# ScalarE instead of SP issues the transfers of the rows of maxima in a cross-attention and expert-FFN kernel

## The chip, the cores and the metric

The kernel runs on one core of one Trainium2 chip. The metric is the device time of one execution in microseconds; less is better. A comparison of two kernels takes the median of several executions of each on the same chip.

## What is computed

The reference handles 8 batches of 512 positions with 256 features. Each batch goes through two stages, each added to its input:

- **An mLSTM cross-attention** with 4 heads of 64: gates from products with the inputs, a cumulated log forget gate, a running maximum, and a decayed product of queries, keys and values.
- **A feed-forward block.** Its first half is a mixture of two multi-head attentions (M = 2, H = 16 heads of KD = 16 each, so 32 heads). For each head it computes

```
scores = q k^T / sqrt(16)        # 512 x 512
attn   = softmax(scores, axis=-1)
ctx    = attn v
```

Its second half picks two of eight experts for the batch and applies them (`gelu(n2 w1) w2`).

The change is about the softmax of the 32 heads. The softmax needs, for each query position, the maximum of its 512 scores. The kernel computes all scores twice: first with queries on the partitions, to take maxima along the free axis, and then with keys on the partitions, where the maximum of a query has to be subtracted in each column.

## The kernel before, in words

**Heads, quads, slots.** Heads are handled four at a time: a quad. A batch has `NQ` = 8 quads. For every quad, TensorE makes 16 tiles of scores with queries on the partitions (`maximum`, line 851), and VectorE reduces each to a column of maxima (line 1378). Then TensorE transposes the 16 columns to 16 rows (`max_rows`, line 859, shown as line 452 of the helper), and VectorE writes them negated, as a high and a low bf16 part, to `mrow` (lines 1386 and 1388). Two DMAs of 4 KB per quad copy these rows from 16 partitions of `mrow` into two rows of the operand `qst` (`send_rows`, line 2009). With these two rows, the second product (`score`, line 866: 98 contraction rows, the last two against ones) comes out of TensorE with the maximum already subtracted, and ScalarE only has to exponentiate it (`exponent`, line 1677) into `prob`. TensorE multiplies `prob` with the values (line 881).

One batch is a **period** of 128 **slots**; a slot is one score tile and one exponential. The scores of quad `qq` use slots 16·`qq` to 16·`qq`+15. A period takes about 167 us here (period 5 runs from 901.6 to 1068.9 us).

**Written-out order.** Each engine has its own program, written out by hand slot by slot. In each period four things run beside the slots: the maxima of the quads to come (the string `AHEAD` says how many tiles per slot), the first stage of the next batch (`stage_a`), the second half of the projections of this batch (`second_half`), and the end of the previous batch with its experts (`stage_c`). Tables such as `ACT_A` and `SP_C` give the slot of each piece on each engine. There are three plans: `FIRST` for period 0, `MIDDLE` for periods 1 to 6, `LAST` for period 7.

**When rows are made and sent.** `rows_at(plan, later)` finds the slot in which the sixteenth maximum of a quad is made and adds `later`. TensorE and VectorE do `max_rows` at `LATER` = 1 slot behind it, and the send stands at `LATER + SENT` = 2 slots behind it. In `MIDDLE` the sends stand at slots 14, 24, 44, 62, 76, 89, 102 (for quads 1 to 7) and 123 (for quad 0 of the next batch). In `FIRST`: 10, 23, 33, 45, 71, 88, 103, 123. In `LAST`: 13, 20, 38, 60, 72, 85, 105.

**SP's queue.** SP issues every DMA of the kernel, 613 in all, strictly in program order, each behind its semaphore waits: the inputs (line 1941), the three parts of the projections into their stacked places in `kst` and `qst` (`stack`, line 1954, twelve DMAs of 128 KB for a pair of pieces), the gates' rows, the expert weights (lines 2025, 2032), the results, and the maxima rows. The first score of a quad waits for the rows:

```
if g == 0 and j == 0:
    e.wait_ge(rows_in[q_ % 2], 32 * (q_ // 2 + 1))
```

**PSUM banks.** Seven banks (`RB`) are taken in turn by everything TensorE makes, in TensorE's program order (`take`). A tile can start only when the engine that reads the tile seven takes earlier in the same bank has let it go (`u.free`). So a reader that is late on one tile stops TensorE seven tiles later, whatever that tile is for.

**ScalarE's program** around a slot is, in this order: the exponential of the slot, then pieces of `second_half`, `stage_c` and `stage_a` that stand at the slot, then (once per quad) the copy of the quad's context (line 1685). Pieces that matter here: `grow0` of `stage_a` (line 1498, reads the tile of the gates, made at line 502), the copies of values (line 1587), and in the last period `copy_columns` (line 1635).

Of the kernel before, what the change touches and what calls it, by code (L numbers as in the profile page):

```python
# [90 lines left out]
def build(nc, d, out):  # L91

    B, S, E = d["x"].shape
# [11 lines left out]
    QUAD = 4  # L105
    NQ = M * H // QUAD
# [3 lines left out]
    KROWS = len(TERMS_K) * KD  # L110
# [4 lines left out]
    with ctx:  # L115
        def sb(name, shape, dt=F32):
            return ctx.enter_context(nc.sbuf_tensor(name, shape, dt))

        def sem(name):
            return ctx.enter_context(nc.semaphore(name))  # L120
# [43 lines left out]
        rows = mid[0:NH].rearrange("p (r s) -> p r s", r=3)  # L164
# [17 lines left out]
        qst = sb("qst", [P, M * H, S], BF16)  # L182
# [6 lines left out]
        mrow = sb("mrow", [QUAD * NT, 2, 2, P], BF16)  # L189
# [73 lines left out]
        rows_in = [sem("rows_in_0"), sem("rows_in_1")]  # L263
# [24 lines left out]
        uses = ring.uses  # L288
# [6 lines left out]
        LATER, SENT = 1, 1  # L295
# [83 lines left out]
        def periods():  # L379

            for b in range(B):
                plan = FIRST if b == 0 else LAST if b == B - 1 else MIDDLE
                yield b, (b - 1 if b > 0 else None), (b + 1 if b + 1 < B else None), plan
# [10 lines left out]
        def behind_maxima(a, first):  # L394

            a.upto(TILES)
            first.upto(-5)
            a.rest()
            first.upto(-2)
# [10 lines left out]
        def place(plan, slot):  # L410

            return sum(map(int, plan["AHEAD"][:slot]))
# [6 lines left out]
        def rows_at(plan, later):  # L419

            return {next(s for s in range(SLOTS) if place(plan, s + 1) >= TILES * q) + later: (q // NQ, q % NQ)
                    for q in range(1, NQ + 1)}
# [1050 lines left out]

        @block.scalar
        def scalar_program(e):
            def stage_a(b):
                for c in range(KC):
                    yield f"kT{c}"
                    u = uses["kT", b, c]
                    e.wait_ge(u.full, u.n)  # L1480
                    e.activation(kT[:, c, :], psum[:, u.bank, :], ACT.Copy).then_inc(u.free, 1)
                for c in range(KC):
                    yield f"qT{c}"
                    u = uses["qT", b, c]
# [3 lines left out]
                if b > 0:  # L1488
                    yield "gpart"
                    u = uses["gparts", b]  # L1490
# [3 lines left out]
                u = uses["gates", b]  # L1494
# [12 lines left out]
                for h in range(NH):  # L1507
                    for c in range(NT):
                        yield f"mask{h}{c}"
                        if h == 0 and c == 0:  # L1510
# [3 lines left out]
                            u = uses["cols", b]  # L1514
# [23 lines left out]
                for c in range(KC):  # L1538
                    yield f"n1T{c}"
                    u = uses["n1T", b, c]  # L1540
# [61 lines left out]
            def second_half(b):  # L1602
                if b == 0:
                    yield "p3"
                    high(b, 3)
                for pt in range(NT // 2 if b == 0 else 0):
                    yield f"pv{pt}"
                    copy_v(b, 0, pt)
                for n in range(len(PIECES) // M, len(PIECES)):
                    yield f"p{n}"  # L1610
                    high(b, n)
                for pt in range(NT // 2):
                    yield f"v{pt}"
                    copy_v(b, 1, pt)

            def stage_c(b):
                for m in range(M):
                    for c in range(KC):
                        yield f"cxT{m}{c}"
                        u = uses["cxT", b, m, c]  # L1620
                        e.wait_ge(u.full, u.n)
                        e.activation(cxT[:, m, c, :], psum[:, u.bank, :], ACT.Copy).then_inc(u.free, 1)
                yield from experts(b)
# [48 lines left out]
            def exponent(b, qq, g, j):  # L1672
                n, u = (b * NQ + qq) * NT + g, uses["score", b, qq, g, j]
                e.wait_ge(u.full, u.n)
                if j == 0 and n > 1:
                    e.wait_ge(valued, n - 1)
                e.activation(prob[:, g % 2, j, :], psum[:, u.bank, :], ACT.Exp).then_inc(u.free, 1)  # L1677
# [12 lines left out]
            until_maxima(a, first)  # L1690
            behind_maxima(a, first)
            for b, behind, ahead, plan in periods():
                a = first if b == 0 else Side(stage_a(ahead) if ahead is not None else iter(()), plan["ACT_A"])
                c = Side(stage_c(behind) if behind is not None else iter(()), plan["ACT_C"])
                v = Side(second_half(b), plan["ACT_S"])
                w = Side(early(b) if ahead is None else iter(()), EARLY_ACT)
                a.upto(-1)
                c.upto(-1)
                for qq in range(NQ):
                    for g in range(NT):  # L1700
                        for j in range(QUAD):
                            slot = (qq * NT + g) * QUAD + j
                            exponent(b, qq, g, j)
                            v.upto(slot)
                            c.upto(slot)
                            a.upto(slot)
                            w.upto(slot)
                            if g == COPY // QUAD and j == COPY % QUAD and b + qq > 0:
                                copy_context(*divmod(b * NQ + qq - 1, NQ))
                if ahead is None:  # L1710
                    copy_context(B - 1, NQ - 1)
                if ahead is not None:
                    c.rest()
                    a.rest()
                else:
                    z = Side(ending(b), ENDING)
                    for slot in range(SLOTS, SLOTS + AFTER):
                        c.upto(slot)
                        z.upto(slot)
# [219 lines left out]
        def sync_program(e):  # L1939
# [65 lines left out]
            def send_rows(b, qq):  # L2005
                u, q_ = uses["rows", b, qq], b * NQ + qq
                e.wait_ge(u.free, u.n)
                for r in range(2):
                    e.dma_start(qst[KROWS + r:KROWS + r + 1, qq * QUAD:(qq + 1) * QUAD, :], mrow[:, q_ % 2, r, :]
                                ).then_inc(rows_in[q_ % 2], 16)  # L2010
# [79 lines left out]
            until_maxima(a, first)  # L2090
            behind_maxima(a, first)
            for b, behind, ahead, plan in periods():
                sends = rows_at(plan, LATER + SENT)
                a = first if b == 0 else Side(stage_a(ahead) if ahead is not None else iter(()), plan["SP_A"])
                c = Side(stage_c(behind) if behind is not None else iter(()), plan["SP_C"])
                v = Side(second_half(b), plan["SP_S"])
                a.upto(-1)
                for slot in range(SLOTS):
                    if slot in sends and b + sends[slot][0] < B:
                        send_rows(b + sends[slot][0], sends[slot][1])  # L2100
                    v.upto(slot)
                    c.upto(slot)
                    a.upto(slot)
                if ahead is not None:
                    c.rest()
                    a.rest()
                else:
                    z = Side(ending(b), ENDING)
                    for slot in range(SLOTS, SLOTS + AFTER):
                        c.upto(slot)  # L2110
                        z.upto(slot)
# [30 lines left out]
```

## Time and profile before

| what | value |
|---|---|
| times of three runs | 1421.33, 1423.33, 1429.55 us |
| median | 1423.33 us |
| span of the profiled execution | 1426.9 us |
| TensorE (PE) busy | 1393.6 us, 98% |
| VectorE (DVE) busy | 1092.2 us, 77% |
| ScalarE (ACT) busy | 916.4 us, 64% |
| GpSimd (POOL) busy | 363.6 us, 25% |
| granted TensorE clock, mean | 0.990 |
| row DMAs (line 2009) | 128 of 4 KB, median 2.1 us from issue to landing |

The page gives no time of the profiled execution beside its span. The span, from the first to the last instruction, lies between the lowest and the highest of the three runs and 3.6 us over their median. In the page, a group of instructions has its busy time, the mean of one in ns, then the idle time of its engine just before it and who ended that. A busy TensorE is not TensorE at its peak, since its matmuls overlap and their ends are modelled: the step from one matmul's start to the next tells more. "SPq" is SP's queue of DMA issues.

### The profile page before, as it was taken

Reading aid. Unit: us, or ns where it says so; the run is one execution under the profiler, and the core shown is the slowest. Engines: PE = TensorE matmul, PEld = TensorE weight load, DVE = VectorE, ACT = ScalarE, POOL = GpSimd, SP = SyncE. Lnnn points to the kernel's source line nnn. Section 1 sums busy time; section 2 is a strip of 40 time slices with the busy share of each in tenths; the row PEclk is TensorE's granted clock in tenths of the full one; section 3 lists DMA queues with packets and bytes.
Section 4 is the critical chain, followed back from the end, with each engine's and each line's share of the span. In section 5 each row is a group of like instructions: output and inputs, shape, how many; then the busy total and the mean of one; then the engine's idle time right before and its main releaser. Section 6 shows DMA issues by size and latency. Waiting matters only on the chain.

```text
span 1426.9 us, 22218 instructions
## 1 busy us (share of the span) xinstructions
PE 1393.6 (98%) x7666; PEld 716.9 (50%) x7666; DVE 1092.2 (77%) x2299; ACT 916.4 (64%) x1706; POOL 363.6 (25%) x351
## 2 busy tenths in 40 slices
PE   8999899999999999999999999999999999999999
PEld 5643434455454654555445554455545454454456
DVE  5779977987789877987779877797769986786721
ACT  3266557766677666675677765876666766757752
POOL 6512342203313123132241133130331322330000
PEclk9999999999999999999999999999999999999999
DMA  4056037430854127441464308541084413561002
GB/s 116 17 70 95 2 45 107 71 62 16 104 76 76 45 38 112 75 75 31 51 101 69 64 31 101 79 75 46 24 102 70 78 56 45 73 77 46 17 1 89
DMA packets 92308, 90.15 MB, mean 63 GB/s; under 512 B 16483, under 2 KB 87267, under 8 KB 91295
## 3 DMA queue, kind: packets, MB, share of 16 engines
q1 hardware_dynamic: 92196, 88.73, 38.6%
q8 instruction: 62, 1.02, 0.3%
q14 instruction: 50, 0.40, 0.1%
HBM read 35.05 MB, written 4.25 MB: 28 GB/s over the span
## 4 chain that ended last, share of the span: by engine, by line
PE 69%; issue 8%; DVE 4%; DMA 3%; SPq 2%; POOL 1%; ACT 1%; DVEq 0%; POOLq 0%; ACTq 0%
PE psum L881 12%; PE psum L866 12%; PE psum L851 12%; PE psum L819 7%; PE psum L838 6%; PE psum L701 5%; PE psum L452 5%; PE psum L736 3%; DMA qst<-mrow 3%; PE psum L475 2%; SPq L1954 2%; PE psum L563 2%; DVE mx L1378 1%; PE psum L573 1%; DVE x L1293 1%
## 5 line engine op out<-in xcount | busy, mean ns | idle before, releaser
L1378 DVE TENSOR_REDUCE mx<-psum 128x1 f32<-128x512 f32 x1024 | 645.5, 681 | 134.2 <-PE psum L851 133.5
L1677 ACT ACTIVATE prob<-psum 128x512 f32<-128x512 f32 x1024 | 568.2, 600 | 270.8 <-PE psum L881 159.4
L866 PE MATMUL psum<-qst,kst 98*128 98x512 bf16 x1024 | 355.9, 383 | 10.5 <-DMA qst<-mrow 8.7
L851 PE MATMUL psum<-kst,qst 96*128 96x512 bf16 x1024 | 318.8, 381 | 2.9 <-DVE resid L1252 1.3
L881 PE MATMUL psum<-prob,vst 128*17 128x512 f32 x2048 | 248.1, 601 | 2.7 <-ACT prob L1677 2.3
L866 PEld LDWEIGHTS psum<-qst,kst 98*128 98x128 bf16 x1024 | 96.9, 99 | 220.8 <-issue 126.9
L851 PEld LDWEIGHTS psum<-kst,qst 96*128 96x128 bf16 x1024 | 99.0, 98 | 121.2 <-issue 17.9
L881 PEld LDWEIGHTS psum<-prob,vst 128*17 128x17 f32 x2048 | 46.7, 97 | 136.3 <-issue 106.8
L838 PE MATMUL psum<-w,cxT 128*128 128x256 f32 x448 | 105.4, 381 | 0.0
L819 PE MATMUL psum<-n2T,x 128*128 128x512 f32 x224 | 103.0, 592 | 0.0
L1828 POOL CAST parts<-resid 128x512 bf16<-128x512 f32 x64 | 41.0, 640 | 239.9 <-DVE resid L1252 239.9
L838 PEld LDWEIGHTS psum<-w,cxT 128*128 128x128 f32 x448 | 85.0, 191 | 16.7 <-DVE acc L1372 1.4
L1748 POOL TENSOR_SCALAR_AFFINE_SELECT cmat<-cmat 128x512 f32<-128x512 f32 x32 | 20.3, 637 | 227.1 <-ACT cmat L1521 227.1
L1830 POOL TENSOR_TENSOR parts<-resid,parts 128x512 bf16<-128x512 f32 x64 | 74.4, 1163 | 5.1
L1798 POOL TENSOR_TENSOR kin<-qbuf,onw 128x1024 f32<-128x1024 f32 (+1 forms) x8 | 16.4, 2054 | 218.2 <-DVE qbuf L1089 216.1
L1724 POOL TENSOR_TENSOR rstd_a<-rstd_a,neghalf 128x4 f32<-128x4 f32 x24 | 25.1, 1055 | 179.4 <-DVE rstd_a L963 109.1
L819 PEld LDWEIGHTS psum<-n2T,x 128*128 128x128 f32 x224 | 42.4, 190 | 39.5 <-issue 34.1
L701 PE MATMUL psum<-n1T,wk 128*128 128x512 f32 x128 | 60.6, 595 | 0.0
L475 PE MATMUL psum<-wv,n1T 128*128 128x256 f32 x256 | 60.5, 379 | 0.0
L701 PE MATMUL psum<-n1T,wq 128*128 128x512 f32 x128 | 60.2, 592 | 0.0
L1599 ACT ACTIVATE parts<-psum,bks 128x512 bf16<-128x512 f32 x32 | 22.0, 687 | 58.4 <-PE psum L701 58.4
L475 PEld LDWEIGHTS psum<-wv,n1T 128*128 128x128 f32 x256 | 48.5, 190 | 9.3 <-ACT prob L1677 0.9
(244 smaller groups left out, 1761.5 us busy)
## 6 DMA issues: line engine op xcount, KB each, us to landing
kst<-parts SPq DMA_DIRECT2D x186, 128.0 KB, 4.7
qst<-parts SPq DMA_DIRECT2D x186, 128.0 KB, 5.9
cmat<-G_dram SPq DMA_DIRECT2D x7, 1024.0 KB, 4.6
x<-in_L_ffn_fw SPq DMA_DIRECT2D x14, 512.0 KB, 3.7
w<-in_L_ffn_fw SPq DMA_DIRECT2D x14, 512.0 KB, 4.2
xbuf<-in_x SPq DMA_DIRECT2D x8, 512.0 KB, 5.1
kin<-in_ctx SPq DMA_DIRECT2D x8, 512.0 KB, 4.5
out<-acc SPq DMA_DIRECT2D x7, 512.0 KB, 9.0
```

What stands on the lines that cost most here:

```text
L452: return e.transpose(out_, in_, ident[0:n, 0:n])
L475: ins = e.matmul(psum[:, u.bank, i * H * KD:(i + 1) * H * KD], n1T[:, kc, t * P:(t + 1) * P], wv[:, kc, m, :], start=kc == 0, stop=kc == K ...
L701: ins = e.matmul(psum[:, u.bank, :], w_[:, kc, m, c * P:(c + 1) * P], n1T[:, kc, :], start=kc == 0, stop=kc == KC - 1)
L736: ins = e.matmul(psum[:, u.bank, 0:E], cxT[:, m, c, t * P:(t + 1) * P], wo[:, m, c, :], start=k == 0, stop=k == M * KC - 1)
L819: ins = e.matmul(psum[:, u.bank, :], w1_of(b, k)[:, kc, f * P:(f + 1) * P], n2T_of(b)[:, kc, :], start=kc == 0, stop=kc == KC - 1)
L838: ins = e.matmul(psum[:, u.bank, 0:E], hidden_of(b, k)[:, f, t * P:(t + 1) * P], w2_of(b, k)[:, f, :], start=f == 0, stop=f == FC - 1)
L851: e.matmul(psum[:, u.bank, :], qst[0:KROWS, h, t * P:(t + 1) * P], kst[0:KROWS, h, :], start=True, stop=True).then_inc(u.full, 1)
L866: e.matmul(psum[:, u.bank, :], kst[0:KROWS + 2, h, g * P:(g + 1) * P], qst[0:KROWS + 2, h, :], start=True, stop=True).then_inc(u.full, 1)
L881: ins = e.matmul(psum[32 * j:32 * j + VW, VB, :], vst[:, g, h, :], prob[:, g % 2, j, :], start=g == 0, stop=g == NT - 1, tile_position=(0, ...
L1378: e.tensor_reduce(mx[:, qq * QUAD + j, t:t + 1], psum[:, u.bank, :], AX, ALU.max).then_inc(u.free, 1)
L1677: e.activation(prob[:, g % 2, j, :], psum[:, u.bank, :], ACT.Exp).then_inc(u.free, 1)
L1830: e.tensor_tensor(parts[:, n % 2, 2, :], resid[:, n % 2, :], parts[:, n % 2, 1, :], ALU.subtract).then_inc(split_lo, 1)
```

## The change

`send_rows` is added to ScalarE's program, with the same wait and the same two DMAs, and stands directly behind the exponential of the slot in which SP had it. SP's loop over slots no longer sends rows. SP keeps the rows of the very first quad, ahead of period 0. Nothing else changes: the number of DMAs, the buffers, the semaphores and all tables of slots are the same.

```
         @block.scalar
         def scalar_program(e):
+            def send_rows(b, qq):
+                u, q_ = uses["rows", b, qq], b * NQ + qq
+                e.wait_ge(u.free, u.n)
+                for r in range(2):
+                    e.dma_start(qst[KROWS + r:KROWS + r + 1, qq * QUAD:(qq + 1) * QUAD, :], mrow[:, q_ % 2, r, :]
+                                ).then_inc(rows_in[q_ % 2], 16)
...
             for b, behind, ahead, plan in periods():
+                sends = rows_at(plan, LATER + SENT)
...
                             exponent(b, qq, g, j)
+                            if slot in sends and b + sends[slot][0] < B:
+                                send_rows(b + sends[slot][0], sends[slot][1])
                             v.upto(slot)
...
         def sync_program(e):
...
-                sends = rows_at(plan, LATER + SENT)
...
                 for slot in range(SLOTS):
-                    if slot in sends and b + sends[slot][0] < B:
-                        send_rows(b + sends[slot][0], sends[slot][1])
                     v.upto(slot)
```

## Rows read from the trace of the kernel before

**Rows 1.** Page, part 1: busy us (share of the span) xinstructions

```profile
PE 1393.6 (98%) x7666; PEld 716.9 (50%) x7666; DVE 1092.2 (77%) x2299; ACT 916.4 (64%) x1706; POOL 363.6 (25%) x351
```

**Rows 2.** Page, part 5: busy us, mean ns | idle before, releaser

```profile
L1677 ACT ACTIVATE prob<-psum 128x512 f32<-128x512 f32 x1024 | 568.2, 600 | 270.8 <-PE psum L881 159.4
L866 PE MATMUL psum<-qst,kst 98*128 98x512 bf16 x1024 | 355.9, 383 | 10.5 <-DMA qst<-mrow 8.7
```

**Rows 3.** TensorE's waits, whole span: us in total, times, longest us

```profile
PE psum L866 <- DMA qst<-mrow: 8.7, 9, 2.9
```

**Rows 4.** The same view from 235 to 1070 us, periods 1 to 5

```profile
PE psum L866 <- DMA qst<-mrow: 4.3, 6, 0.9
```

**Rows 5.** Waits of SP's queue, whole span, same columns

```profile
SPq L2009 <- DVE mrow L1388: 346.1, 51, 28.1
```

**Rows 6.** Line L2009, min/median/max: issue (ns), issue to landing (us)

```profile
L2009 SPq DMA_DIRECT2D qst<-mrow x128: 502/584/1826, 81.0 to 1353.7; - x128
...
DMA to landing us min/median/max: 1.6/2.1/5.8
```

**Rows 7.** Timeline, period 5, slot 89: start us, us, instruction, [idle before]

```profile
1031.46 0.28 DVE L1388 SCALAR_TENSOR_TENSOR mrow<-psum,mrow 16x128 bf16<-16x128 f32 x1
1031.79 3.83 SPq L1954 DMA_DIRECT2D kst<-parts  x6
...
1032.43 2.83 ACT L1677 ACTIVATE prob<-psum 128x512 f32<-128x512 f32 x5 [0.71 <-PE psum L881]
...
1035.67 1.23 SPq L2009 DMA_DIRECT2D qst<-mrow  x2
...
1042.14 0.39 PE L866 MATMUL psum<-qst,kst 98*128 98x512 bf16 x1 [0.88 <-DMA qst<-mrow]
```

**Rows 8.** Timeline of period 5 around slot 14

```profile
921.37 1.05 PE L502 MATMUL psum<-cmat,wsum 128*36 128x512 f32 x2
...
922.35 0.28 PE L452 MATMUL psum<-ident,mx 128*16 128x128 f32 x1
...
922.46 0.38 PE L866 MATMUL psum<-qst,kst 98*128 98x512 bf16 x1
...
922.68 0.81 PE L851 MATMUL psum<-kst,qst 96*128 96x512 bf16 x3
923.04 0.57 ACT L1677 ACTIVATE prob<-psum 128x512 f32<-128x512 f32 x1
...
923.33 3.62 PE L736 MATMUL psum<-wo,cxT 128*128 128x256 f32 x16
923.63 0.68 ACT L1498 ACTIVATE cmat<-psum,gbias 4x512 f32<-4x512 f32 x1
...
924.08 0.28 DVE L1388 SCALAR_TENSOR_TENSOR mrow<-psum,mrow 16x128 bf16<-16x128 f32 x1
```

**Rows 9.** Timeline of period 5 around slot 123

```profile
1064.71 3.16 ACT L1677 ACTIVATE prob<-psum 128x512 f32<-128x512 f32 x6 [0.94 <-PE psum L881]
...
1066.23 0.28 DVE L1388 SCALAR_TENSOR_TENSOR mrow<-psum,mrow 16x128 bf16<-16x128 f32 x1
...
1067.76 0.58 SPq L1941 DMA_DIRECT2D kin<-in_ctx  x1
...
1068.29 0.60 ACT L1587 ACTIVATE vst<-psum 128x512 f32<-128x512 f32 x1 [0.42 <-PE psum L475]
...
1069.31 1.06 ACT L1677 ACTIVATE prob<-psum 128x512 f32<-128x512 f32 x2
...
1069.94 0.09 PEld L866 LDWEIGHTS psum<-qst,kst 98*128 98x128 bf16 x1 [0.29 <-ACT prob L1677]
```

**Rows 10.** Timeline of the last period around slot 85

```profile
1340.10 0.59 ACT L1635 ACTIVATE kin<-psum 128x512 f32<-128x512 f32 x1
...
1340.47 0.28 DVE L1388 SCALAR_TENSOR_TENSOR mrow<-psum,mrow 16x128 bf16<-16x128 f32 x1
...
1340.97 0.60 PE L866 MATMUL psum<-qst,kst 98*128 98x512 bf16 x2
```

More of the change, by code:

```diff
@@ L1475, in scalar_program, with send_rows @@
         def scalar_program(e):
+            def send_rows(b, qq):
+                u, q_ = uses["rows", b, qq], b * NQ + qq
+                e.wait_ge(u.free, u.n)
+                for r in range(2):
+                    e.dma_start(qst[KROWS + r:KROWS + r + 1, qq * QUAD:(qq + 1) * QUAD, :], mrow[:, q_ % 2, r, :]
+                                ).then_inc(rows_in[q_ % 2], 16)
             def stage_a(b):
@@ L1692, in scalar_program @@
             for b, behind, ahead, plan in periods():
+                sends = rows_at(plan, LATER + SENT)
                 a = first if b == 0 else Side(stage_a(ahead) if ahead is not None else iter(()), plan["ACT_A"])
@@ L1703, in scalar_program @@
                             exponent(b, qq, g, j)
+                            if slot in sends and b + sends[slot][0] < B:
+                                send_rows(b + sends[slot][0], sends[slot][1])
                             v.upto(slot)
@@ L2092, in sync_program @@
             for b, behind, ahead, plan in periods():
-                sends = rows_at(plan, LATER + SENT)
                 a = first if b == 0 else Side(stage_a(ahead) if ahead is not None else iter(()), plan["SP_A"])
@@ L2098, in sync_program @@
                 for slot in range(SLOTS):
-                    if slot in sends and b + sends[slot][0] < B:
-                        send_rows(b + sends[slot][0], sends[slot][1])
                     v.upto(slot)
```

## The prediction

> **What bounds the kernel now.** I read the page first. TensorE is busy 98% of the span, VectorE 77%, ScalarE 64% [rows 1]. So a time can only be gained where TensorE stands still, and it is lost wherever ScalarE or a transfer makes it stand still once more. The costliest groups show where ScalarE has room: before its 1024 exponentials it is idle 270.8 us, mostly because TensorE is not ready [rows 2]. The same part shows what the rows of maxima cost today: 8.7 us of TensorE's idle time before `score` ends with their transfer. The view of TensorE's waits says how these lie: nine waits, the longest 2.9 us [rows 3]; six of them with 4.3 us together fall between 235 and 1070 us [rows 4]. This is the largest entry that TensorE has. It is also all that earlier rows can give back.
>
> Why are they late? SP stands in `send_rows` for 346.1 us in all, waiting for VectorE [rows 5], and that is harmless. The timeline around slot 89 shows the harmful case [rows 7]. VectorE ends `mrow` at 1031.74. SP has just begun a stack of six DMAs and reaches the rows at 1035.67, 3.9 us late. They then land behind 128 KB transfers, and the first score of the quad starts at 1042.14, after 0.88 us of idling. The shape is the same in each middle period.
>
> **What the change takes away.** 126 issues leave SP. At slot 89 ScalarE can issue by 1033, since the five exponentials that begin at 1032.43 include that of slot 89 as the second [rows 7]. That is 2.7 us earlier. Even if the rows then still took the 6.4 us from issue to use that they take now (1035.67 to 1042.1), they would be there at 1039.4, before the 1041.2 at which TensorE asks. With the median landing of 2.1 us [rows 6] they are there by 1036. I take all nine waits as gone: **-8.7 us**. The least is 5, if the long one of period 0 (2.9 us) stays in part.
>
> SP runs ahead where it stood in `send_rows`. At slot 123 the loads of the next batch go out at 1067.76, behind the rows [rows 9]; they will go out up to ten microseconds earlier. TensorE does not wait for them now, so nothing is gained: 0. What could be lost is that they share the DMA engines with the rows of slot 123, whose quad starts as they land; 0 to 0.5 us in seven periods. I take 0, because the loads start long enough before the rows to be nearly done.
>
> **What it adds.** A pair of issues occupied SP for 1.18 us (median 584 ns for one [rows 6]; 1.23 in [rows 7]). No row shows ScalarE issuing a DMA. The bounds are 0, if its work in progress covers the issue, and 1.83 us per issue, the longest of SP's. I take SP's 1.18 us a pair, the nearest row, during which nothing behind the pair can begin. 63 pairs make 74 us; as ScalarE waits 270.8 us for TensorE, most of it is hidden by those waits. Without that cover each pair costs its 1.2 us. What counts is where TensorE follows closely on ScalarE. The program order gives these places, and the timeline their slack:
>
> **Slot 14, six middle periods.** Behind the exponential of slot 14 stands the read of the gates' tile, line 1498. It began at 923.63 and ended at 924.31 [rows 8]. The send now stands between them and waits for `mrow`, which ends at 924.36: the change adds a wait here too. Then come 1.18 us, so line 1498 begins at 925.6 and ends at 926.3, 2.0 us late. Who needs it? The gates' bank comes round again seven takes after line 502: the transposed maxima, one score, three maxima, the first product tile of line 736, the second. Sixteen matmul records lie at 0.216 us ((3.62 - 0.38) / 15), eight a tile, so the second tile began at 923.33 + 8 x 0.216 = 925.06. It will begin 0.15 us after 926.3, at 926.45. Loss: 1.4 us, six times: **+8.4 us**. This is the one price that the table of slots hands to the change.
>
> **Slot 123, seven periods.** `mrow` ends at 1066.51, the pair holds ScalarE until 1067.7, and the exponential behind it, which began at 1066.77, begins 1.0 us later. ScalarE's 0.42 us of idling before line 1587 absorbs part, so the exponentials at 1069.31 are 0.5 us late [rows 9]. The next weight load follows straight upon ScalarE (0.29 us of idling ended by it): 0.4 us, seven times: **+2.8 us**.
>
> **Slot 24, six periods.** Here a run of eight exponentials without a gap follows, and 0.75 us of delay (1.18 plus the restart, less the 0.49 us step of exponentials) is carried through it. TensorE gets about half by its seven banks: 0.4 us, six times: **+2.4 us**. This is an estimate from the run of slot 123, not read from a row; its ends are 0 and 0.75.
>
> **Slots 44, 62, 76, 89, 102.** `mrow` is done before the exponential or just as it begins, and ScalarE is then about to wait for TensorE: 0. If the cover is thin, 0.3 us each, 9 us over six periods; that goes into the upper end.
>
> **First and last period.** At slot 85 of the last one, line 1635 begins at 1340.10 and TensorE's matmul at 1340.97 follows 0.28 us behind its end. `mrow` ends at 1340.75, so line 1635 begins at 1342.0, 1.9 us late: 1.8 us on TensorE [rows 10]. Period 0 has two or three tight places of this kind (ends of `mrow` at or behind the exponential at slots 33 and 45), which I put at 1.0 to 1.5 us each by the two places worked out; with small ones in the last period I take 5.6 us for both periods: **+5.6 us**, between 2 and 9.
>
> **Sum:** 8.4 + 2.8 + 2.4 + 5.6 - 8.7 = +10.5 us against the span of 1426.9. The median of the runs is 3.6 us under the span; I put the same difference on the median: 1423.3 + 10.5 = 1433.8, rounded to **1434 us**.
>
> **Against a rule.** The transfers are not the point here; what the issue costs against its transfer is. The pair costs its issuer 1.18 us while the transfer takes 2.1 us [rows 6], so the cost of issuing is more than half of the transfer. The Trainium skill, "DMA: Bandwidth & Descriptors", section "Issuing engines are not separate DMA queues", says that issuing on several engines saves only the sequencer's time, which is usually small relative to the DMA. For 4 KB the trace does not agree with the second half; taken as it stands, that rule would let the +19.2 us vanish and the gain with it shrink to what SP's lateness caused.
>
> **The rivals.**
> *A. ScalarE is not held up.* Work already handed to it goes on while the DMAs are issued, so only the wait for `mrow` is left. Then the prices fall and the 8.7 us stay as gain, less about 4 us for slots 14 and 85, where the wait alone delays lines 1498 and 1635 by 0.7 us: 1423.3 - 8.7 + 4 = 1418.6, and 1414.6 if that is covered as well. For it: runs of exponentials start every 0.5 us although each lasts 0.6 [rows 2], [rows 9], so something is ahead. Against it: most of ScalarE's time before exponentials is spent waiting, so little is in hand, and it cannot begin what has not been handed over. It decides if the pair holds ScalarE for under 0.6 us. The Trainium skill, "Advanced Engine Details and Errata", section "Engine Queue Depths", gives ScalarE a queue of 8, which would favour this rival; no row shows how full it is.
> *B. The issue is dearer on ScalarE,* because SP issues at the same time. At 0.9 us each a pair costs 0.6 more. All the places above (6 + 7 + 6 + about 5) rise by that 0.6, 14 us, less the two microseconds that still hide: 1423.3 + 10.5 + 12 = 1446. For it: the longest issue of SP took 1826 ns [rows 6].
> *C. It comes out even.* The bank order leaves more slack than I count, and slot 14 alone costs: 8.4 + 1.8 - 8.7, or 1425. For it: ScalarE is idle a fifth of the span before exponentials [rows 2].
> *D. The change does nothing,* the rows go out at the same moments. Slot 89 speaks against it; it would give 1423 and falls to C.
>
> **How the numbers follow.** 0.5% of 1423.3 is 7.1 us, about what a measurement of this kernel can tell from no change; so the bounds are 1416.2 and 1430.4. Forecast (1428 to 1440): 0.58. A: 0.14, a third of it below 1416.2. B: 0.12. C and D: 0.16. Faster: 0.05 of A and a little for the unseen, 0.07. Slower: B 0.12, and 0.52 of the forecast's 0.58, 0.64. Same: the rest, 0.29. The range leaves out the low half of A and the high half of B: 1418 to 1446.
>
> **What would show it.** DMA issues of rows on ScalarE's queue of 0.5 to 0.6 us each; no wait of TensorE for `qst<-mrow` at slot 89; line 1498 beginning 2 us later relative to the exponential of slot 14, and TensorE idle before the second tile of line 736 with ScalarE as the releaser; middle periods longer by about 1.2 us each (2.2 lost, 1.0 won). I am wrong if pairs last under 0.6 us or if ScalarE begins work during them, if line 736 has no gap, or if new waits for the rows appear at slot 123.

## The result, and the profile after

| | before | after |
|---|---|---|
| median, same chip | 1422.36 us | 1512.31 us |
| all runs | 1421.33 to 1429.55 | 1510.2 to 1514.29 |
| span of the profiled execution | 1426.9 us | 1510.5 us |
| mean granted TensorE clock | 0.990 | 0.969 |

The ratio is 1.0624, 95% interval 1.06 to 1.0647: slower by 90 us. The forecast was 1434 us, range 1418 to 1446. The direction was right, and the size was off by a factor of eight.

Of the page of after, these lines of parts 1, 3 and 5 (busy us, count; queue, packets, MB, share; busy us, mean ns | idle before, releaser) answer to [rows 1, 2]. The line numbers have moved with the change: the exponential of line 1677 is line 1684 here, the read of the gates' tile 1505 (was 1498), the stacks 1964 (was 1954), the loads 1951 (was 1941), and the send, which was line 2009, is line 1480.

```profile
PE 1423.1 (94%) x7666; PEld 717.2 (47%) x7666; DVE 1089.0 (72%) x2299; ACT 915.3 (61%) x1706; POOL 363.7 (24%) x351
...
q1 hardware_dynamic: 88164, 88.21, 37.8%
q10 hardware_dynamic: 4032, 0.52, 0.3%
...
L1684 ACT ACTIVATE prob<-psum 128x512 f32<-128x512 f32 x1024 | 569.9, 601 | 344.1 <-PE psum L881 203.7
L866 PE MATMUL psum<-qst,kst 98*128 98x512 bf16 x1024 | 359.9, 388 | 51.3 <-DMA qst<-mrow 48.0
```

Two things stand out. The same 7666 matmuls keep TensorE busy 29.5 us longer (1423.1 against 1393.6), while its busy *share* falls from 98% to 94%: it is both slower at its work and idle more. And the wait which the change was to remove has grown from 8.7 to 48.0 us. `q10` is new: 126 of the 128 row transfers are now on ScalarE's own queue.

The view of TensorE's waits (us in total, times, longest) puts two entries ahead of all others; [rows 3] has the first of them before:

```profile
PE psum L866 <- DMA qst<-mrow: 48.0, 16, 4.9
PE psum L736 <- ACT cmat L1505: 7.8, 6, 2.3
```

The second is the price of slot 14, which was forecast. The first was forecast to go to zero. The issues themselves are as cheap as forecast; line 1480 in the view by line (min/median/max of an issue in ns, then of issue to landing in us), against [rows 6]:

```profile
L1480 ACTq DMA_DIRECT2D qst<-mrow x126: 510/604/1766, 103.4 to 1437.5; - x126
...
DMA to landing us min/median/max: 1.6/2.5/9.9
```

So ScalarE issues the rows on time and quickly, and some of them then take up to 9.9 us instead of 5.8 at most. Which ones follows from TensorE's idle time before the first score of each quad. In the six middle periods, 26.9 of the 48.0 us stand before the quad whose rows go out at slot 102 (3.9 to 4.9 us each time) and 13.0 us before that of slot 24 (1.8 to 2.9 us). Another 3.5 and 1.4 us stand before quad 1 of the first and the last period, and 2.8 us before quad 6 of the first period, where the kernel before had 2.9 us already. At slot 123 there is no wait over 0.15 us.

The timeline of period 5 around slot 102 shows such a case (start us, us, instruction, [idle before <- releaser]):

```profile
1109.84 3.78 SPq L1964 DMA_DIRECT2D qst<-parts  x6
...
1111.63 0.28 DVE L1388 SCALAR_TENSOR_TENSOR mrow<-psum,mrow 16x128 bf16<-16x128 f32 x1
...
1111.94 1.31 ACTq L1480 DMA_DIRECT2D qst<-mrow  x2
...
1113.66 0.59 SPq L1951 DMA_DIRECT2D kin<-in_ctx  x1
...
1122.35 0.61 PE L866 MATMUL psum<-qst,kst 98*128 98x512 bf16 x1 [4.77 <-DMA qst<-mrow]
...
1123.18 0.63 PE L866 MATMUL psum<-qst,kst 98*128 98x512 bf16 x1
```

SP started a stack of six 128 KB transfers at 1109.84, 2.1 us ahead of the rows. In the kernel before it was the other way round, since SP itself had to wait for `mrow` and send the rows first. This is the timeline of before at the same slot of the same period:

```profile
1051.43 0.28 DVE L1388 SCALAR_TENSOR_TENSOR mrow<-psum,mrow 16x128 bf16<-16x128 f32 x1
...
1051.74 1.18 SPq L2009 DMA_DIRECT2D qst<-mrow  x2
...
1053.02 3.81 SPq L1954 DMA_DIRECT2D qst<-parts  x6
```

There the two rows took at most 4.2 us to land. In after they took 9.1 and 9.8 us, as the view of line 1480 in this stretch says:

```profile
DMA to landing us min/median/max: 9.1/9.4/9.8
```

The landings lie in the order of issue across the two queues: the stack's fourth transfer, issued at 1111.72 by SP, landed at 1120.99; ScalarE's first row, issued at 1111.94, at 1120.99 too; the stack's fifth, issued at 1112.37, at 1122.01. From one 128 KB transfer to the next about 1.1 us pass, so each of them that goes out ahead of the rows holds them up by about 1.1 us: for the second row, five of them on top of the 4.2 us of the kernel before make 9.7 us, and it took 9.8. (For the first, four on top of 3.5 us make 7.9, and it took 9.1, so the 1.1 us are an estimate.) The Trainium skill, "DMA: Bandwidth & Descriptors", section "Issuing engines are not separate DMA queues", says that DMAs run on the same 16 engines whoever issues them; the trace agrees. The same page of the Trainium skill, section "Queues, rings and completion order", lets each DMA engine take turns between queues, packet by packet. One would expect from it that 4 KB need not wait for a backlog of the other queue; the 9.8 us do not show that. The profile's view of the DMA queues from 1111.9 to 1117.9 us has no packet of `q10` at all, so the rows stood for 6 us before any of their packets moved. Where in the path from the issue to the packets they stood, no run here tells.

Why was TensorE slower at its work as well? Three stretches from 1117 to 1136 us by windows (us, then busy us of PE, PEld, DVE, ACT, POOL with counts, granted clock, DMA share, GB/s):

```profile
1117.00:1122.00 5.00, 0.58 (x3) 0.10 (x1) 1.74 (x3) 1.49 (x4) 2.89 (x2) 0.99 1.17 124
1122.00:1129.00 7.00, 6.65 (x24) 1.47 (x25) 1.32 (x2) 1.89 (x4) 0.00 (x0) 0.52 0.47 132
1129.00:1136.00 7.00, 7.00 (x44) 3.57 (x42) 4.53 (x11) 5.20 (x11) 0.00 (x0) 1.00 0.00 1
```

TensorE stands still for 4.8 us, and when it resumes the granted clock is 0.52, the 1.2 GHz level: 24 matmuls in 7 us, where the next 7 us hold 44. The step from one matmul to the next is 0.42 us (1122.76 to 1123.18 above) instead of 0.22. The starts of the scores give the price: from the first score of this quad to the fourth behind it 6.71 us pass, where the kernel before takes 3.69. So a stall of 5 us here costs some 8. Over the six middle periods the stretch behind slot 102's wait is 2.1 us longer on average than before. Adding up the half-clock stretches of both traces gives 27 us before and 92 us after.

### The profile page after: what moved, and what is told of

The parts are those of the page before. It is cut to its first block, busy times and chain, and to the rows that moved or that the text cites. A ratio compares the mean times of both kernels' runs of the same rounds, so it can differ in the third digit from the quotient of the medians.

```text
span 1510.5 us, 22218 instructions
## 1 busy us (share of the span) xinstructions
PE 1423.1 (94%) x7666; PEld 717.2 (47%) x7666; DVE 1089.0 (72%) x2299; ACT 915.3 (61%) x1706; POOL 363.7 (24%) x351
## 4 chain that ended last, share of the span: by engine, by line
PE 66%; issue 8%; DMA 7%; ACT 4%; DVE 3%; POOL 1%; ACTq 1%; DVEq 0%; POOLq 0%
PE psum L881 13%; PE psum L866 11%; PE psum L851 11%; DMA qst<-mrow 7%; PE psum L838 7%; PE psum L701 6%; PE psum L819 6%; PE psum L452 4%; ACT prob L1684 3%; PE psum L736 2%; PE psum L563 2%; PE psum L475 1%; DVE mx L1378 1%; ACTq L1480 1%; PE psum L573 1%
## 5 line engine op out<-in xcount | busy, mean ns | idle before, releaser
L866 PE MATMUL psum<-qst,kst 98*128 98x512 bf16 x1024 | 359.9, 388 | 51.3 <-DMA qst<-mrow 48.0
L851 PE MATMUL psum<-kst,qst 96*128 96x512 bf16 x1024 | 325.5, 386 | 7.6 <-issue 2.2
L881 PE MATMUL psum<-prob,vst 128*17 128x512 f32 x2048 | 264.7, 636 | 2.6 <-ACT prob L1684 2.3
L736 PE MATMUL psum<-wo,cxT 128*128 128x256 f32 x224 | 53.6, 381 | 7.8 <-ACT cmat L1505 7.8
L701 PE MATMUL psum<-n1T,wq 128*128 128x512 f32 x128 | 60.2, 592 | 0.0
```

The source lines that it names most:

```text
L701: ins = e.matmul(psum[:, u.bank, :], w_[:, kc, m, c * P:(c + 1) * P], n1T[:, kc, :], start=kc == 0, stop=kc == KC - 1)
L736: ins = e.matmul(psum[:, u.bank, 0:E], cxT[:, m, c, t * P:(t + 1) * P], wo[:, m, c, :], start=k == 0, stop=k == M * KC - 1)
L851: e.matmul(psum[:, u.bank, :], qst[0:KROWS, h, t * P:(t + 1) * P], kst[0:KROWS, h, :], start=True, stop=True).then_inc(u.full, 1)
L866: e.matmul(psum[:, u.bank, :], kst[0:KROWS + 2, h, g * P:(g + 1) * P], qst[0:KROWS + 2, h, :], start=True, stop=True).then_inc(u.full, 1)
L881: ins = e.matmul(psum[32 * j:32 * j + VW, VB, :], vst[:, g, h, :], prob[:, g % 2, j, :], start=g == 0, stop=g == NT - 1, tile_position=(0, ...
```

## The experiments

Three theories stood after the result. **SP ahead** (theory 1): the old place of `send_rows` in SP's queue was a brake; without it SP puts its stacks and loads in front of the rows. **A worse queue** (theory 2): a transfer from ScalarE's own queue is served worse beside SP's. **The hold** (theory 3): ScalarE, held for 1.2 us a pair, is later than forecast everywhere. All ratios are against the kernel before on the same chip. The edits are against after where nothing else is said.

**1. SP waits for `mrow` again at every old place**, but sends nothing (`e1_gate`):

```
+                sends = rows_at(plan, LATER + SENT)
                 for slot in range(SLOTS):
+                    if slot in sends and b + sends[slot][0] < B:
+                        u = uses["rows", b + sends[slot][0], sends[slot][1]]
+                        e.wait_ge(u.free, u.n)
                     v.upto(slot)
```

> ScalarE sends the rows as in the changed kernel, but SP still waits for mrow at each of its old places (it issues nothing there), so it runs ahead no more. Theory 1 (SP, no longer held, queues 128 KB transfers and loads ahead of the rows): TensorE's wait for the rows falls from 48 us to under 8, and the time to about 1434 us, which is before plus what holding ScalarE costs. Theory 2 (a transfer from ScalarE's own queue is served worse beside SP's): it stays at 1490 us or more, with landings of 6 us and more at slots 24 and 102. Theory 3 (the hold of ScalarE is the main cost): it stays at 1490 or more with short landings.

Measured: 1493.59 us, ratio 1.0471 (1.0429 to 1.0512). TensorE's waits:

```profile
PE psum L866 <- DMA qst<-mrow: 30.4, 18, 3.8
PE psum L736 <- ACT cmat L1505: 9.0, 6, 2.3
```

Only 19 of the 90 us came back. By its time alone this is theory 2 or 3, and the 1434 us of theory 1 are missed. The landings part them: at slot 24 the rows now take 4.1 to 4.6 us in the middle periods (5.4 to 6.5 in after), at slot 102 5.0 to 6.2 us (8.9 to 9.9), and TensorE's waits there fall from 40.0 to 5.6 us. The loss moved to slot 123. The gate reopened SP at the very moment at which ScalarE began to issue, so both issued side by side. The rows of slot 123, whose second lands 2.3 us behind the first issue in after, now needed 4.3 to 6.2 us, mostly 5.5, beside the loads of the next batch, and stopped TensorE six times, for 1.9 to 3.8 us, 18.0 us in all. Being after `mrow` is not enough. That SP's transfers must come behind the rows' *issue*, as they did when one queue held both, is the reading that experiments 5 and 9 try.

**2. The same gate for the rows of quads 2 and 7 alone** (slots 24 and 102, where stacks stand next in SP's program; `e2_gate_2_7`): the condition of experiment 1 gets `and sends[slot][1] in (2, 7)`.

> The changed kernel, with SP's wait for mrow put back at two of eight places only: quads 2 and 7, slots 24 and 102 of the middle plan. Theory 1: these two places carry nearly all the loss of the middle periods, so the time is 1435 to 1450 us. If running ahead hurts everywhere (the loads behind slot 123 among it), it is 1470 or more. Theories 2 and 3: as before the gate, near 1512.

Measured: 1462.71 us, ratio 1.0281 (1.0244 to 1.0318); waits for rows 14.3 us, 14 times. That is 13 us over theory 1's range and far from theories 2 and 3. Two gates bring back 50 us, more than eight did, since the loads behind slot 123 are left where after has them: long ahead of the rows.

**3. The hold alone** (`e3_spare`): the kernel *before*, whose SP sends the rows as ever, and ScalarE issues as many further pairs into rows of `qst` that nobody reads.

```
+            def send_spare(b, qq):
+                u, q_ = uses["rows", b, qq], b * NQ + qq
+                e.wait_ge(u.free, u.n)
+                for r in range(2):
+                    o = KROWS + 4 + q_ % 2 * 2 + r
+                    e.dma_start(qst[o:o + 1, 0:QUAD, :], mrow[:, q_ % 2, r, :]).then_inc(spare_in[q_ % 2], 16)
...
                             exponent(b, qq, g, j)
+                            if slot in sends and b + sends[slot][0] < B:
+                                send_spare(b + sends[slot][0], sends[slot][1])
```

VectorE waits for `spare_in` before it overwrites `mrow`.

> The kernel before, with SP sending all rows, and ScalarE issuing the same pairs once more, to unused rows of qst, at the places of the changed kernel. This is the hold of ScalarE by itself (and a doubled 4 KB traffic). My sum of places gives +19 us: 1440 to 1444 us, 8 us of it before the second tile of line 736 in six periods. Theory 3: 1490 or more. If ScalarE is not held, 1423.

Measured: 1450.99 us, ratio 1.0186 (1.0153 to 1.0218): **+28 us**. The lines of its page and of its waits (every line number of TensorE is one higher here):

```profile
PE 1397.0 (96%) x7666; PEld 712.3 (49%) x7666; DVE 1098.6 (76%) x2299; ACT 915.7 (63%) x1706; POOL 363.5 (25%) x351
```

```profile
PE psum L867 <- DMA qst<-mrow: 12.9, 15, 3.9
PE psum L737 <- ACT cmat L1508: 7.8, 6, 2.3
```

Against these lines, after has 35.1 us more of waits for rows (48.0 - 12.9) and 26.1 us more of busy TensorE (1423.1 - 1397.0, the half clock behind the stalls). Together that is 61.2 us, and the medians differ by 61.3. (The spans of the two profiled executions differ by 60.2.) So the 90 us split into 28 for the hold and 61 for the rows that come late. The split is by subtraction here; experiments 6 and 9 make 55.6 of the 61 us appear and vanish. The 28 us are not pure either: the spare transfers double the 4 KB traffic, and TensorE's waits for the real rows, still sent by SP, are 4.2 us longer than before (12.9 against 8.7). Up to that much of the 28 us is traffic and not hold.

**4. Only quad 6 from ScalarE** (`e4_quad6`), the one send where SP was really late (slot 89, [rows 7]); SP sends all others.

```
-                            if slot in sends and b + sends[slot][0] < B:
+                            if slot in sends and sends[slot][1] == 6:
                                 send_rows(b + sends[slot][0], sends[slot][1])
...
+                sends = rows_at(plan, LATER + SENT)
                 for slot in range(SLOTS):
+                    if slot in sends and b + sends[slot][0] < B and sends[slot][1] != 6:
+                        send_rows(b + sends[slot][0], sends[slot][1])
```

> ScalarE sends only quad 6 of each batch (slot 89 of the middle plan), where SP is late; SP sends the other seven. The waits of about 1 us at slot 89 and the one of 2.9 us in period 0 go: theory 1 gives 1414 to 1419 us. If a row transfer from ScalarE's queue is served worse as such (theory 2), it lands late here too and nothing is gained: 1423 or more.

Measured: 1424.34 us, ratio 1.0003 (0.9984 to 1.0022). The waits at slot 89 are gone from the middle periods (the rows land about 4 us before TensorE asks), and the total is lower:

```profile
PE psum L866 <- DMA qst<-mrow: 5.9, 7, 2.8
```

Yet no time is won, and the expected 1414 to 1419 us are missed. The 2.9 us wait of period 0 stayed (2.8). By the starts of the quads' first scores, the stretch up to quad 6 is 0.86 us shorter in each middle period and the stretch behind it 0.65 us longer. There the maxima of the next quad wait for a stack that lands no earlier than before: in period 2 its last transfer lands at 545.38 us, and the maximum starts at 545.47 after 0.34 us of idling. Only the place of the wait changed.

**5. The gate lets SP go on only when the rows of quads 2 and 7 have landed** (`e5_landed`): as experiment 2, but SP waits on `rows_in` for `32 * (q_ // 2 + 1)`.

> The changed kernel, with SP waiting at quads 2 and 7 until their rows have landed, so that none of its later transfers can share the DMA engines with them. With a wait for mrow alone at these places (1462.7 us) the rows still took 4.6 to 6 us. Theory 1 in its sharper form (rows lie in one line with whatever SP issued before them or at the same moment): landings at slot 24 fall to about 3.5 us, its wait goes, and the time is what holding ScalarE costs, 1450 to 1457 us. If ScalarE's queue is served worse by itself, nothing changes: 1460 or more.

Measured: 1456.77 us, ratio 1.025 (1.023 to 1.0271); waits for rows 13.5 us, 9 times. 6 us better than experiment 2, and within the range expected: at slot 24 the rows land in 1.7 to 3.3 us in the middle periods. What is left is 5.8 us above experiment 3. This sits outside the middle periods: no gate guards quad 1 of the first and last period, where TensorE waits 3.5 and 1.5 us, and at slot 123 of period 0 it waits 3.2 us.

**6. Only quads 2 and 7 from ScalarE, with no gate** (`e6_quads27`): as experiment 4 with `in (2, 7)` in the place of `== 6`, so that a quarter of the pairs is moved.

> ScalarE sends only quads 2 and 7 of each batch; SP sends, and is held at, the six others. The quarter of the change that theory 1 blames. The segments of the changed kernel behind the start of quads 1, 2, 6 and 7 are longer than those of the kernel with spare pairs by 2.1, 1.3, 4.6 and 1.8 us in each middle period, 59 us in six, so about 1475 to 1490 us. Theory 3 (holding ScalarE), with a quarter of the pairs: 1430.

Measured: 1483.67 us, ratio 1.0425 (1.04 to 1.0451), and TensorE's first wait:

```profile
PE psum L866 <- DMA qst<-mrow: 45.1, 22, 4.4
```

16 of the 63 pairs, a quarter of the change, carry two thirds of its loss.

**7. Another order on SP alone** (`e7_order`): the kernel before, but the stack of slot 89 stands behind the rows of quad 6 in `SP_A` (`G:65 s0:16` becomes `G:74 s0:7`; in `FIRST` `G:54 s0:21` becomes `G:68 s0:7`), and the results' transfer behind slot 102 (`w21:30` becomes `w21:32`).

> SP sends all rows as before; only SP's slots change: the stack s0 stands behind the rows of quad 6 (slot 89, in period 0 slot 88) and the result's transfer behind those of quad 7 (slot 103). This takes SP's lateness of 3.9 us at slot 89 without holding ScalarE. If the waits at slot 89 can be won at all: 1414 to 1419 us. If the DMA engines are full from slot 89 to 105, so that stacks come later by what the rows come earlier (as in the run with quad 6 on ScalarE, where a maximum then waited for a stack): 1421 to 1425.

Measured: 1431.32 us, ratio 1.0061 (1.0037 to 1.0085). No wait for rows is left among TensorE's largest; these have come instead:

```profile
PE psum L851 <- issue: 7.4, 6, 2.0
PE psum L851 <- DMA qst<-parts: 6.8, 1, 6.8
```

The expectation was missed. Line 851, which makes the maxima, needs the stack, and in the middle periods what the rows gain the stack loses: the stretch up to quad 6 is 0.86 us shorter, the one behind it 1.56 us longer. In period 2 the stack's last transfer lands at 547.52 us and the maximum that waited starts at 547.62. The 6.8 us are one wait in period 0, where the stack was moved too, and they are most of the 8.5 us by which this kernel is slower. With experiment 4 this says that neither reordering wins the 8.7 us of [rows 3].

**8. Only the wait on ScalarE** (`e8_wait`): the kernel before, and ScalarE waits for `mrow` at each place and issues nothing.

> The kernel before; ScalarE only waits for mrow at the 63 places, and issues nothing. It parts the wait from the hold in the +28 us of the spare pairs. From the rows: at slot 14 line 1498 comes 0.75 us later, which its slack of 0.6 us nearly covers; the same at slot 85 of the last period. So 1423 to 1428 us, and the rest, over 20 us, is the issuing itself.

Measured: 1424.46 us, ratio 1.002 (1.0006 to 1.0034). So of the 28 us of experiment 3 the wait makes about 2 (1 to 5 by the interval), and the rest comes with the issues.

**9. Experiment 6, with SP kept back until these rows have landed** (`e9_quads27_landed`):

```
+                sends = rows_at(plan, LATER + SENT)
                 for slot in range(SLOTS):
+                    if slot in sends and b + sends[slot][0] < B and sends[slot][1] not in (2, 7):
+                        send_rows(b + sends[slot][0], sends[slot][1])
+                    elif slot in sends and b + sends[slot][0] < B:
+                        q_ = b * NQ + sends[slot][1]
+                        e.wait_ge(rows_in[q_ % 2], 32 * (q_ // 2 + 1))
```

> As the run in which ScalarE sends the rows of quads 2 and 7 alone (1483.67 us, +60 us, 45.1 us of waits for rows), but SP waits at the two slots until these rows have landed before it goes on to its stack. Theory (the cost is SP running ahead, so that its 128 KB transfers stand in front of the rows): the rows land within 2 to 4 us of their issue, TensorE's waits for rows fall below 15 us, and 1425 to 1438 us. Rival (ScalarE issues these rows too late, or its queue is slow for them): the waits stay over 30 us and the time at 1460 us or more.

Measured: 1428.06 us, ratio 1.0034 (1.0022 to 1.0047). The same 32 issues of ScalarE at the same slots; only SP's place has changed, and 55.6 us are gone (1483.67 - 1428.06). TensorE's first wait, then the landing of all 32 (6 had 1.7/5.6/9.4):

```profile
PE psum L866 <- DMA qst<-mrow: 9.7, 11, 3.0
```

```profile
DMA to landing us min/median/max: 1.6/1.8/4.5
```

And the timeline around slot 102, where the stack now comes 3.6 us behind the rows:

```profile
1047.00 0.28 DVE L1388 SCALAR_TENSOR_TENSOR mrow<-psum,mrow 16x128 bf16<-16x128 f32 x1
1047.31 1.17 ACTq L1480 DMA_DIRECT2D qst<-mrow  x2
...
1050.92 3.11 SPq L1964 DMA_DIRECT2D qst<-parts  x5
```

Neither ScalarE's queue nor the moment of its issue is at fault, which rules out theory 2 for these rows. This settles the larger part: 55.6 us are SP ahead at quads 2 and 7, and the 5 us that remain over the kernel before are what 16 pairs on ScalarE, with SP held back for them, cost.

**10. Experiment 3 without the spare pair of quad 1** (slot 14; `e10_spare_not1`): the condition gets `and sends[slot][1] != 1`, and the counts of `spare_in` follow.

> As the run with the kernel before and spare pairs from ScalarE (1450.99 us, +28 us), without the spare pair of quad 1, which stands at slot 14 in the six middle periods (and at the same place of the first and last). Theory (a held ScalarE costs where matmuls wait for its G cast): the 7.8 us of TensorE's waits for ScalarE's cmat go, and the time is 1438 to 1444 us. Rival (the hold costs the same wherever it stands, 28 us over 8 quads of a period): 1446 to 1449 us.

Measured: 1444.88 us, ratio 1.0148 (1.0125 to 1.017). The 7.8 us of waits for the gates' tile have left the list, and 6.1 us of the 28 are gone. The time does not decide: it lies between the theory's 1438 to 1444 and the rival's 1446 to 1449, and its four runs reach from 1442.38 to 1446.27. The starts of the quads' first scores decide for the theory: the stretch with slot 14 was 1.56 us longer than before in each middle period of experiment 3 and is as long as before here. The other seven pairs of a period cost 22 us over the kernel, about 3 us each on average.

**11. All but quads 2 and 7 from ScalarE** (`e11_not27`): experiment 6 turned round, `not in (2, 7)` on ScalarE and `in (2, 7)` on SP.

> The complement of that run: ScalarE sends all rows but those of quads 2 and 7, which SP sends as before. Theory (SP ahead does harm only where stacks stand behind the rows; elsewhere only the hold on ScalarE costs, 28 us over all pairs): 1440 to 1452 us, TensorE's waits for rows under 15 us. Rival (running ahead does harm at every pair, 90 us less 60 us of it being a chance split): over 1455 us with waits for rows over 20 us.

Measured: 1451.44 us, ratio 1.0205 (1.0179 to 1.0232), in four runs from 1443.05 to 1456.15; the profiled one has a span of 1441.3, so its lines stand for the low end. TensorE's waits:

```profile
PE psum L866 <- DMA qst<-mrow: 11.0, 7, 3.5
PE psum L736 <- ACT cmat L1505: 6.9, 6, 1.4
```

Its +29 us and the +61 of experiment 6 add up to the 90 of the whole change, though the four runs spread too widely (25 to 33 us by the interval) to make much of the agreement. The rival is not wholly wrong: before quad 1 of the first and last period TensorE waits 3.5 and 1.4 us here, as in after, where the kernel before has 0.6 and nothing. There too SP puts a stack in front of the rows that it used to send first (period 0: six transfers of `qst` from 102.45 us on, rows from 103.4). So about 55 of the 61 us lie at quads 2 and 7 and some 6 us outside them.

No version beat the kernel before; experiment 4 equals it.

## Why the prediction was right in its direction and wrong in its size

**The step that failed** stands in the part on what the change takes away: "SP runs ahead where it stood in `send_rows`." It was put at 0, as a gain and as a loss, with 0 to 0.5 us in seven periods as the bound of the loss. It looked only at the loads behind slot 123, and these turned out harmless in after: they go out so early that they have landed when the rows come (2.3 us to landing there). It did not go through the other seven sends and ask what stands *next* in SP's program. Behind slot 102 it is the stack of `qst` and then the loads of 512 KB; behind slot 24 three transfers of a `kst` stack. The 346.1 us that SP spent waiting in `send_rows` [rows 5] were called harmless. They were, as a delay, but they were also what kept the order. The term was 0 and measured 61 us (after against experiment 3), 55.6 of them at quads 2 and 7 alone: 1483.67 us with SP ahead, 1428.06 without (experiments 6 and 9). The prediction's own sign of being wrong looked for new waits at slot 123 and at no other send.

**The step on the gain, -8.7 us, fell with it.** "Even if the rows then still took the 6.4 us" was a bound taken from a queue that sent them first. At slot 89 it held: issued at 1093.54, they had landed by 1098.1, 4 us before TensorE asked. At slots 24 and 102 it did not. Of the nine waits that were taken as gone, the six at slot 89 went, and the 2.9 us of period 0 stayed. And where it held it was worth nothing on its own (experiment 4), because the stack that follows had become the next to be late. Where that stall would go, and what would be late next, was not asked for slot 89.

**What held.** The direction was not luck: experiment 3, where the hold acts by itself, is slower than before, as the sum had it. The larger cause of the loss, though, stood in the sum at 0. The price of an issue on ScalarE, taken from SP's row (584 ns), measured 604. Slot 14 was right in mechanism and size: +8.4 forecast, 7.8 us of waits in six places, with this timeline in period 5 of after:

```profile
979.05 0.57 ACT L1684 ACTIVATE prob<-psum 128x512 f32<-128x512 f32 x1
...
980.40 1.15 ACTq L1480 DMA_DIRECT2D qst<-mrow  x2
981.60 0.68 ACT L1505 ACTIVATE cmat<-psum,gbias 4x512 f32<-4x512 f32 x1 [1.98 <-issue]
...
982.34 1.99 PE L736 MATMUL psum<-wo,cxT 128*128 128x256 f32 x8 [1.10 <-ACT cmat L1505]
```

The read of the gates' tile begins 1.2 us behind the issue's start, the exponential before it having ended at 979.62, just as worked out for [rows 8]. Taking it away brought 6.1 us by the medians, and 9.5 us by the starts of the quads in the six middle periods of the profiled executions.

**The rest of the hold was mis-sized.** The sum for it was 8.4 + 2.8 + 2.4 + 5.6 = 19.2 us, and experiment 3 measured 28. By the starts of the quads' first scores, the middle periods lose 3.3 us each there instead of the forecast 2.2. The stretch with slot 14 loses 1.56 us (forecast 1.4) and the one with slot 123 0.31 (0.4). The two with slots 24 and 44 lose 1.07 us together, where 0.4 was forecast for slot 24 and 0 for slot 44; in experiment 9, where ScalarE does not send at slot 44, they still lose 0.71, so slot 24 lies near the 0.75 that the prediction gave as its upper end. The stretch with slot 102 loses 0.58, of which 0.41 are waits for SP's rows beside the spare ones, so not the hold. The three with slots 62, 76 and 89 lose between -0.27 and 0.17. The first and last period lose 6.9 us (forecast 5.6). The reserve of 0.3 us on each of the five sends put at 0 would have brought the sum to 28, but the loss is not spread that way. No send but that of slot 14 was tried by itself, nor was the whole change with SP held back at every send.

Rival A (ScalarE is not held up) is refuted in its price by experiment 8 against experiment 3: the wait alone costs about 2 us, and with the issues it is 28. Its premise is half right. The timeline of ScalarE at slot 89 in period 5 of after has the exponential of slot 89 itself, handed over before the pair, running from 1093.98 us while the issues run from 1093.54 to 1094.70:

```profile
1093.54 0.52 ACTq L1480 DMA_DIRECT2D qst<-mrow  x1
1093.98 0.59 ACT L1684 ACTIVATE prob<-psum 128x512 f32<-128x512 f32 x1
1094.09 0.61 ACTq L1480 DMA_DIRECT2D qst<-mrow  x1
1094.75 1.57 ACT L1684 ACTIVATE prob<-psum 128x512 f32<-128x512 f32 x3 [0.18 <-PE psum L866]
```

What stands behind the pair starts only when the issues have ended, at 1094.75. Here that costs little, since the issues began beside a running exponential; at slot 14 they could begin only 0.8 us behind its end. Rival B (a dearer issue) did not occur (604 ns, not 900). Rival C (only slot 14 costs) is refuted by experiment 3, and D (nothing moves) by slot 89, where the rows left SP's place and went out earlier.

**The rule cited.** The prediction cites the Trainium skill, "DMA: Bandwidth & Descriptors", section "Issuing engines are not separate DMA queues", for issuing being usually small relative to the DMA. For 4 KB that did not hold: an issue took 604 ns against a landing of 2.5 us at the median, and 63 pairs cost up to 28 us. The more useful half of that section, that all issuers share the DMA engines, was not drawn on. It was the half that mattered.

**The clock** had no place in the sum. In the middle periods of the kernel before only one stall, of 0.95 us in period 3, is followed by a half-clock stretch (3.4 us). In after a stretch of 3.4 or 6.8 us follows each of the twelve stalls of 1.8 to 4.9 us at slots 24 and 102. TensorE's busy time puts this at up to 26.1 of the 61 us; no run took the stalls and left the clock, so the share is a reading of the traces.

## What to carry to other kernels

A wait in a DMA queue that looks idle may be what puts the transfers in order. Before a DMA moves to another engine, list for *each* place what stands next in the old queue, when it could go out without the wait, and how many bytes it then puts in front of the moved transfer. If the move is wanted, make the old queue wait for the moved transfer's landing, not for its input. On a compute engine count each issue as time in which nothing behind it starts (0.6 us here), and don't count a stall as won until it is known what ends the wait that follows it.

## What the hardware showed that was not expected

- Two 4 KB transfers from ScalarE's queue landed in the order of issue among SP's 128 KB transfers, 9.8 us after their issue, with about 1.1 us for each large one ahead. A second queue was no way round a backlog.
- Issuing on two queues at the same moment (experiment 1, slot 123) is enough to raise the time from the first issue to the landing of both 4 KB rows from 2.3 to 5.5 us; the other queue's transfers were two of 512 KB.
- While ScalarE issued DMAs, an exponential handed over before them ran on (1093.98 us, between the issues of 1093.54 and 1094.09); the next one waited for their end.
- After a stall of 4.8 us TensorE ran at the 1.2 GHz level for most of 7 us (clock 0.52, 24 matmuls against 44), so the stall cost about 3 us more than its own length. In the whole kernel the stretches at that level grew from 27 to 92 us.
